# Router logits scaled inside attention by a row of scales read back from DRAM, and two gated tiles finished by VectorE in the experts

## The reference

```python
x = x + tanh(g_xattn) * cross_attention(layernorm(x), ctx)   # 4 heads, 64 context tokens
x = x + tanh(g_ffn)   * experts(layernorm(x))
# experts, on groups of 32 tokens (n groups, t = 32), 32 experts x 4 sets = 128 columns
logits = einsum('bntd,des->bntes', grouped, Wc) + bc + tie
perm   = (logits == max(logits over t))                      # each expert picks one token of a group
inner  = relu(einsum(picked, W1) + b1)
result = einsum(inner, W2) + b2, scattered back with perm
```

## Time and profile before

| | |
|---|---|
| median of 3 runs | 1808.31 us (1807.01 to 1816.78) |
| profiled execution, its own time | 1809.33 us |
| its span | 1807.4 us |
| granted TensorE clock, mean | 0.971 |
| busy share PE / PEld / DVE / ACT / POOL | 91% / 63% / 71% / 42% / 48% |
| chain that ended last, by engine | PE 59%, DVE 11%, issue 10%, DMA 9%, POOL 8% |
| of it, DMA `gat<-r_scratch` / POOL L1219 / POOL L184 | 6% / 4% / 2% |
| DMA | 324.81 MB, mean 180 GB/s |

### The profile page before, as it was taken

One profiled execution on the slowest core, in us unless ns is written; L12 is line 12 of the kernel. 1 busy time (PEld: TensorE's weight loads), 2 busy tenths in 40 slices (PEclk: granted clock), 3 DMA queues, 4 the chain that ended last, 5 costly groups with the idle time before them and its releaser, 6 DMA issues.

```text
span 1807.4 us, 51758 instructions
## 1 busy us (share of the span) xinstructions
PE 1648.8 (91%) x22488; PEld 1146.4 (63%) x22488; DVE 1278.0 (71%) x1856; ACT 754.4 (42%) x995; POOL 858.6 (48%) x1016
## 2 busy tenths in 40 slices
PE   7899999999999999999779988888888888889896
PEld 4677777777777777777545665456644566445663
DVE  5677777777777777777537777666766767666676
ACT  3533232332333323322245545555455554555553
POOL 3467777767777677776322223332223322333213
PEclk9999999999999999999889999999899999999998
DMA  7534444444443445444457778786678766788666
GB/s 274 161 108 151 168 156 148 137 163 143 156 158 131 163 146 177 140 149 138 145 191 198 227 179 219 213 218 206 173 210 229 215 207 175 213 226 227 204 182 164
DMA packets 180882, 324.81 MB, mean 180 GB/s; under 512 B 23344, under 2 KB 33328, under 8 KB 179248
## 3 DMA queue, kind: packets, MB, share of 16 engines
q1 hardware_dynamic: 135728, 239.68, 40.5%
q0 software_dynamic: 17280, 31.46, 10.7%
q10 hardware_dynamic: 27648, 50.34, 8.1%
HBM read 242.71 MB, written 78.71 MB: 178 GB/s over the span
## 4 chain that ended last, share of the span: by engine, by line
PE 59%; DVE 11%; issue 10%; DMA 9%; POOL 8%; ACT 2%; SPq 1%; ACTq 1%; POOLq 0%; DVEq 0%
PE ps L1385 13%; PE ps L877 10%; PE ps L924 10%; PE ps L1358 7%; DMA gat<-r_scratch 6%; PE ps L937 5%; POOL out L1219 4%; PE ps L892 3%; PE ps L950 2%; DVE mx L675 2%; POOL xin L184 2%; PE ps L911 2%; PE ps L1408 2%; DVE lg L679 1%; DVE sm L684 1%
## 5 line engine op out<-in xcount | busy, mean ns | idle before, releaser
L184 POOL TENSOR_SCALAR xin<-xin,r_all,nb_all 128x512 f32<-128x512 f32 x128 | 97.9, 771 | 505.2 <-DMA xin<-out 505.1
L1298 DVE STREAM_TRANSPOSE res<-res 128x2048 f32<-128x2048 f32 x128 | 292.1, 2295 | 0.1
L1249 ACT ACTIVATE gat<-ps 128x1536 f32<-128x1536 f32 (+1 forms) x128 | 171.3, 1345 | 215.6 <-PE ps L1358 215.5
L1314 DVE COPY res<-ps 128x1024 f32<-128x1024 f32 x128 | 155.3, 1223 | 92.0 <-PE ps L1408 92.0
L877 PE MATMUL ps<-xTh,qh 128*128 128x512 f32 x512 | 208.9, 408 | 5.6 <-DVE qs L692 1.9
L877 PE MATMUL ps<-xTh,ql 128*128 128x512 f32 x512 | 200.3, 391 | 0.0
L877 PE MATMUL ps<-xTl,qh 128*128 128x512 f32 x512 | 200.0, 391 | 0.0
L1358 PE MATMUL ps<-sel,xin 32*128 32x128 f32 x4096 | 158.2, 293 | 37.4 <-POOL xin L184 17.2
L1263 ACT ACTIVATE res<-ps 128x1024 f32<-128x1024 f32 x128 | 131.2, 1025 | 143.6 <-PE ps L1408 143.6
L532 POOL TENSOR_TENSOR qc<-qc,qs 128x512 f32<-128x512 f32 x64 | 82.6, 1290 | 208.8 <-DVE qs L692 208.8
L1358 PEld LDWEIGHTS ps<-sel,xin 32*128 32x128 f32 x4096 | 135.7, 197 | 50.6 <-issue 25.5
(11 more groups left out here) (156 smaller groups left out, 3376.3 us busy)
## 6 DMA issues: line engine op xcount, KB each, us to landing
gat<-in_W ACTq DMA_DIRECT2D x192, 256.0 KB, 6.6
xT<-in_xT SPq DMA_DIRECT2D x32, 1024.0 KB, 6.2
xin<-in_x SPq DMA_DIRECT2D x64, 512.0 KB, 3.8
out<-xin SPq DMA_DIRECT2D x64, 512.0 KB, 3.8
xin<-out SPq DMA_DIRECT2D x128, 256.0 KB, 4.5
xin<-in_W SPq DMA_DIRECT2D x128, 256.0 KB, 3.5
out<-xin POOLq DMA_DIRECT2D x120, 256.0 KB, 7.6
xT<-in_W SPq DMA_DIRECT2D x68, 256.0 KB, 4.4
```

The costliest lines, as they stand in the source:

```text
L184: e.tensor_scalar(self.xn[:, t, :], self.xn[:, t, :], self.r[:, i, t:t + 1], self.nb[:, i, t:t + 1], ALU.mult, ALU.add).then_inc(self.m_xn ...
L1249: e.activation(o, v, ACT.Copy).then_inc(m_gaA.sem, 1)
L1298: e.transpose(v, v).then_inc(m_tr.sem, 1)
L1314: e.tensor_copy(o, v).then_inc(m_evV.sem, 1)
```

## The change

One more slot for `lx` (three), a buffer `rrow` for the scales in attention, and `rowk` moves from the stage-wide constants to the experts. SyncE's `store_r` becomes `logits_out`: it stores r, waits for that, loads r back from DRAM broadcast to all partitions, waits for GpSimd's product, and stores the scaled logits. In the experts the load of r and the product are gone, and VectorE makes tiles 0 and 1 of `finish` between its picks.

```diff
+LX_RING = 3
     def load_logits(self, e, i, h):
-        v = self.room(i, h)
-        e.dma_start(v[:, 0:HT], self.lg_dram[i, h]).then_inc(self.d_lg[h].sem, 16)
-        e.dma_start(v[:, HT:2 * HT], self.r_dram[i, h].rearrange("p t -> (p t)").partition_broadcast(P)).then_inc(self.d_lg[h].sem, 16)
+        e.dma_start(self.room(i, h)[:, 0:HT], self.lg_dram[i, h]).then_inc(self.d_lg[h].sem, 16)
...
-    def scaled(self, e, i, h):
...
-            e.wait_ge(self.m_lr.sem, self.m_lr.at(i, h))
+            e.wait_ge(self.d_lg[h].sem, self.d_lg[h].at(i))
...
-        lx = sb("lx", [P, 2, HT])
+        lx = sb("lx", [P, LX_RING, HT])
+        rrow = sb("rrow", [P, HT])
...
         def sync(e):
-            def store_r(u):
-                e.wait_ge(route.m_r.sem, route.m_r.at(u // 2, u % 2))
-                e.dma_start(route.r_dram[u // 2, u % 2], route.r[:, u // 2, u % 2 * TH:(u % 2 + 1) * TH]).then_inc(d_r.sem, 16)
+            def logits_out(u):
+
+                i, h = u // 2, u % 2
+                e.wait_ge(route.m_r.sem, route.m_r.at(i, h))
+                e.dma_start(route.r_dram[i, h], route.r[:, i, h * TH:(h + 1) * TH]).then_inc(d_r.sem, 16)
+                e.wait_ge(d_r.sem, d_r.at(u))
+                e.dma_start(rrow[:], route.r_dram[i, h].rearrange("p t -> (p t)").partition_broadcast(P)).then_inc(d_rr.sem, 16)
+                e.wait_ge(m_lsr.sem, m_lsr.at(u))
+                e.dma_start(route.lg_dram[i, h], lx[:, u % LX_RING, :]).then_inc(d_lgs[u % LX_RING].sem, 16)
...
-                e.wait_ge(m_ls.sem, m_ls.at(u))
-                e.dma_start(route.lg_dram[u // 2, u % 2], lx[:, u % 2, :]).then_inc(d_lgs[u % 2].sem, 16)
...
                     if h and u:
-                        store_r(u - 1)
+                        logits_out(u - 1)
...
-            store_r(NU - 1)
+            logits_out(NU - 1)
...
-            for k in range(2):
-                e.wait_ge(d_lgs[k].sem, d_lgs[k].at(B - 1))
-            e.wait_ge(d_r.sem, d_r.at(NU - 1))
+            for k in range(LX_RING):
+                e.wait_ge(d_lgs[k].sem, d_lgs[k].at((NU - 1 - k) // LX_RING))
...
         def gpsimd(e):
+            def scaled_logits(u):
+                o = lx[:, u % LX_RING, :].rearrange("p (t s) -> p t s", s=P)
+                e.wait_ge(m_ls.sem, m_ls.at(u))
+                e.wait_ge(d_rr.sem, d_rr.at(u))
+                e.tensor_tensor(o, o, rrow[:].rearrange("p (s t) -> p t s", t=TH), ALU.mult).then_inc(m_lsr.sem, 1)
...
                                         rc[:, tp, :].unsqueeze(2).broadcast_to([P, 8, S]), ALU.mult).then_inc(m_pr.sem, 1)
+                if unit(g - 2):
+                    scaled_logits(g - 2)
                 if unit(g + 1):
                     rotated(g + 1, 0)
...
-                if g == NU - 1:
-                    route.scaled(e, 0, 0)
-                    route.scaled(e, 0, 1)
                 if g >= NU - 2:
                     for t in range(TH):
                         route.normed(e, 0, (g - NU + 2) * TH + t)
+            scaled_logits(NU - 2)
             row_scale(NU - 1)
+            scaled_logits(NU - 1)
...
             def part_of_x(u):
                 e.wait_ge(m_LX.sem, m_LX.at(u))
-                if u >= 2:
-                    e.wait_ge(d_lgs[u % 2].sem, d_lgs[u % 2].at(u // 2 - 1))
-                e.activation(lx[:, u % 2, :], ps[:, 7, :], ACT.Copy).then_inc(m_lx.sem, 1)
+                if u >= LX_RING:
+                    e.wait_ge(d_lgs[u % LX_RING].sem, d_lgs[u % LX_RING].at(u // LX_RING - 1))
+                e.activation(lx[:, u % LX_RING, :], ps[:, 7, :], ACT.Copy).then_inc(m_lx.sem, 1)
...
+        def finish(e, i, t):
+
+            e.wait_ge(m_sc.sem, m_sc.at(i, t))
+            if t < 2:
+                e.tensor_scalar(tile_of(t), ps[:, 4 + t % 4, :], gate_f[:], None, ALU.mult).then_inc(m_finV.sem, 1)
+            else:
+                e.activation(tile_of(t), ps[:, 4 + t % 4, :], ACT.Copy, scale=gate_f[:]).then_inc(m_fin.sem, 1)
...
-                    route.scaled(e, i + 1, 0)
-                    route.scaled(e, i + 1, 1)
...
                         for h in range(2):
-                            for step in range(3):
-                                pick(i + 1, h, step)
+                            pick(i + 1, h, 0)
+                            if live(i - 1) and h == 0:
+                                finish(e, i - 1, 0)
+                            pick(i + 1, h, 1)
+                            if live(i - 1) and h == 0:
+                                finish(e, i - 1, 1)
+                            pick(i + 1, h, 2)
```

More of the change, by code:

```diff
@@ L91, in build @@
         b2s = sb0("b2s", [P, 2, D], F32R)
-        rowk = sb0("rowk", [P, 4, P], F32R)
         part = sb0("part", [P, 18])
         tie = sb0("tie", [P, G])
-        consts = (bcol, b1r, b2s, rowk, part, tie)
+        consts = (bcol, b1r, b2s, part, tie)
         const_loads = [(bcol, bc), (tie, tie_in.partition_broadcast(P)), (part, part_in)]
@@ L162, in __init__ @@
         self.d_x = [mark(f"x{t}", 1, 16) for t in range(NT)]
-        self.d_lg, self.m_r = [mark(f"dlg{h}", 2, 16) for h in range(2)], mark("r", 2)
-        self.m_xn, self.m_lr, self.m_log, self.m_mx, self.m_eq = mark("xn", NT), mark("lr", 2), mark("log", 2), mark("mx", 2), mark("eq", 2)
+        self.d_lg, self.m_r = [mark(f"dlg{h}", 1, 16) for h in range(2)], mark("r", 2)
+        self.m_xn, self.m_log, self.m_mx, self.m_eq = mark("xn", NT), mark("log", 2), mark("mx", 2), mark("eq", 2)
         self.m_sT, self.m_sel = mark("sT", 2), mark("sel", 2)
@@ L238, in attention @@
     nhalf, none_, eps_l, eps_r = small
-    b2s, rowk, part = consts[2:5]
+    b2s, part = consts[2:4]
     st = ExitStack()
@@ L333, in attention @@
         m_vcp, m_vce = pmark("vcp", NC), pmark("vce", NC)
-        d_vc, d_lgs, d_r = mark("dvc", 1, 16), [mark(f"lgs{k}", 1, 16) for k in range(2)], mark("dr", 1, 16)
-        m_vch, m_vcl, m_LX, m_LP, m_lx, m_ls = (mark(n) for n in ("vch", "vcl", "LX", "LP", "lx", "ls"))
+        d_vc, d_lgs, d_r, d_rr = mark("dvc", 1, 16), [mark(f"lgs{k}", 1, 16) for k in range(LX_RING)], mark("dr", 1, 16), mark("drr", 1, 16)
+        m_vch, m_vcl, m_LX, m_LP, m_lx, m_ls, m_lsr = (mark(n) for n in ("vch", "vcl", "LX", "LP", "lx", "ls", "lsr"))
         m_s1, m_ag1, m_r1 = mark("s1", TH), mark("ag1"), mark("r1", 3)
@@ L1056, in experts @@
         NY = TH
-        bcol, b1r, b2s, rowk, part, tie = consts
+        bcol, b1r, b2s, part, tie = consts
         xn = route.xn
@@ L1062, in experts @@
         res = sb("res", [P, Q * D])
+        rowk = sb("rowk", [P, 4, P], F32R)
         spare = lambda i: gat[:, 1, i % 2 * UW:(i % 2 + 1) * UW]
@@ L1073, in experts @@
         m_gaA, m_hr, m_evA = mark("gaA", 2 * C), mark("hr", 8), mark("evA", 8)
-        m_gaV, m_evV, m_tr, m_fin = mark("gaV", 2 * C), mark("evV", 8), mark("tr", 8), mark("fin", NT)
+        m_gaV, m_evV, m_tr, m_fin = mark("gaV", 2 * C), mark("evV", 8), mark("tr", 8), mark("fin", NT - 2)
         d_last = mark("last", 4, 16)
         m_gate, m_add, m_end = mark("gate", 3), mark("add", 3), mark("end", 2)
+        m_row = mark("row")
+        m_finV = mark("finV", 2)
         m_xn, m_sel = route.m_xn, route.m_sel
@@ L1143, in copied, with finished @@
             e.wait_ge(m_evV.sem, m_evV.at(i, u))
+        def finish(e, i, t):
[4 more added lines that the diff above has]
+                e.activation(tile_of(t), ps[:, 4 + t % 4, :], ACT.Copy, scale=gate_f[:]).then_inc(m_fin.sem, 1)
+        def finished(e, i, t):
+            m, k = (m_finV, t) if t < 2 else (m_fin, t - 2)
+            e.wait_ge(m.sem, m.at(i, k))
         def load_second(e, i, u, c):
@@ L1268, in scalar @@
                         copy(i, n)
+                    if i == 0:
+                        e.activation(rowk[:].rearrange("p u (k n) -> p (u k) n", k=4), part[:, 0:16].unsqueeze(2).broadcast_to([P, 16, NG]),
+                                     ACT.Copy).then_inc(m_row.sem, 1)
                     for c in range(QUARTERS):
@@ L1276, in scalar @@
                 for t in range(NT):
-                    if live(i - 1) and i < B:
-                        finish(i - 1, t)
+                    if live(i - 1) and i < B and t >= 2:
+                        finish(e, i - 1, t)
                     if live(i) and t < QUARTERS:
@@ L1327, in vector @@
                         for h in range(2):
-                            for step in range(3):
-                                pick(i + 1, h, step)
+                            pick(i + 1, h, 0)
[5 more added lines that the diff above has]
+                            pick(i + 1, h, 2)
+                    elif u == 0 and live(i - 1) and i < B:
+                        for t in range(2):
+                            finish(e, i - 1, t)
                     if live(i):
@@ L1415, in scatter @@
                 if t >= 4:
[L1416 removed]
+                    finished(e, i, t - 4)
                 elif t == 0 and live(i + 1):
```

19 lines of the change are left out of this document (5 added, 14 removed).

## The result

The changed kernel takes 1887.69 us (median of 4 runs, 1885.88 to 1898.05), the kernel before 1807.66 us (4 runs, 1799.24 to 1816.78). The ratio is 1.045, interval 1.039 to 1.052: slower by 80 us. The forecast was slower by 35, 1843 us, and its range ended at 1880. The direction was right, the size was not.

What follows compares the result with a forecast made beforehand. TensorE's order was taken to bound attention; in the experts, TensorE near its limit alternated with late GpSimd products and DMA. Attention +71, hand-over +15, experts -51 on 1809.3 gave 1844, put at 1843 for the median; range 1803 to 1880.

Steps and rivals of the forecast that it cites:

- No slack in the third slot: Attention: the logits copy waits within one turn for r, its DRAM trip, product and store; 29 copies wait, +71 us.
- wait-hidden rival: Attention: the third slot does give a unit of slack, leaving +15 - 51, 1772 us; chance 0.04.
- A to rotation: Attention: from A, the start of ScalarE's copy of the logits, to the rotation, now A+4.4 instead of A+5.0.
- rotation to r: Attention: 12.8 us from rotation until r is made, at A+17.2, up to 0.7 later in units with the `vol` part.
- r's landing: Attention: r lands in DRAM behind the x store on the same queue, 0.7 earlier than A+21.0, at A+20.3.
- store of the logits: Attention: the 256 KB store after the product takes 2.0 us, then the copy starts again at A+24.15+L.
- L: Attention: time of the broadcast load of r's row from DRAM, taken as 3.3 us, between 2.6 and 4.2.
- product: Attention: GpSimd's scaling of the logits after the row load, 1.65 us and 0.05 of release.
- The clock as a second cause: Rival "more on both sides": attention +97 with L 4.2, TensorE's clock low after idling, experts -36; 1886 us, chance 0.07.
- Hand-over: Attention to experts: two round trips of r now precede the load of ring[1], +15 us (13.5 to 16.7).
- long L: Attention: the row load at 4.2 us, making attention +97 us.
- Experts: Two loads, two GpSimd products and their wait go per batch; 3.6 us each for 14, 1 for the last: -51 (-23 to -88).

Runs made afterwards that it cites:

- experiment 2: Changed kernel with ten more TensorE matmuls, results unused, per unit where it waits for the copy of the logits; 1891.71 us, 1.048 of the kernel before.
- experiments 4 and 5: Changed kernel with x's second-half store behind r's store and row load: 1846.24 us; changed kernel with only a quarter of turned x loaded in later units: 1843.52 us.
- experiment 7: The changed kernel's experts on the attention of the kernel before, logits stored unscaled; 1764.99 us, 0.977 of the kernel before.

## Why the prediction missed

- **No slack in the third slot: right.** 29 copies were released by the store, unit by unit. The wait-hidden rival is out.
- **A to rotation, rotation to r: right.** 17.2 forecast, 17.4 measured; the difference is the `vol` part in every second unit, which the sum named and did not add.
- **r's landing: this step failed.** It was put as "Everything ahead of it on the queue moves with the rotation or with `values`, 0.6 to 1.0 earlier; I take 0.7: A+20.3." Measured: A+21.5. The 1.2 us are three pieces: 0.3 since the one unit I read (r at A+21.0) was better than the mean before (A+21.3), 0.7 of expected gain that did not come, and 0.2 later still. Times 29, that is 34 of the 38.5 missing us; most of the rest is the store of the logits, 2.16 where the sum had 2.0. The x store ahead of r was issued 0.7 earlier, as said (at A+12.7, 13.4 before), only in 12 units, all with TensorE at 1.00; in the 16 at 0.94 it went out 0.9 later, at A+14.3. Over all 29 it landed at A+21.1 (A+20.9 before). Even an earlier issue is not an earlier landing: experiment 2 has the issue 0.7 earlier and no gain, and experiments 4 and 5 show that the landing is set by the 512 KB store and the 1 MB load in flight together.
- **L, product: right.** L was 3.3 in the mean, as taken, between 2.6 and 4.2. The Trainium skill, DMA: Bandwidth & Descriptors, "Anatomy of one DMA", comes to an estimate of 2.6 for the size; that section's figures are for DMAs that GpSimd issues, and this load is SyncE's. The shortest of the 32 row loads in the changed kernel took 3.0. The end of 4.2 was real as well, at the hand-over (4.43 and 4.04) and wherever r's store was quick.
- **The clock as a second cause: the symptom right, the price open.** The prediction allowed for slow matmuls after TensorE's idle time, as "1 to 2 us of that fit behind the loop, more would show". They did show: at 0.94 the `values` matmuls end later, the x store goes out later, and the unit is 1.1 us longer, 16 times; an estimate from these means is 18 us of the missing 38.5, inside the late landing above. Yet with the clock held up (experiment 2) the time did not change, so no run shows these 18 us given back. The Trainium skill, TensorE: Matmul & The Clock Gate, "HAM oscillation", has it that a kernel that idles in every turn can be throttled in every turn; the trace agrees in part, with 16 turns of 29. That 1886 was this rival's number is luck: its L of 4.2 and its 36 us from the experts did not come.
- **Hand-over: right,** +16.7 for 15. **Experts: right in the mechanism,** -52.5 for -51; the scatter-to-gather stretch was put at about 25 and took 25.02. The accumulating DMAs took longer to land than the 6 to 8 given, and the start 8 us sooner paid for it. That the sum came within 2 us is in part luck, as experiment 7 shows (34 to 47 us). The two loads' bytes stand in the prediction at 1.4 us a batch and then as 1.6 in the range; only the range's -23 hangs on that.
- **The range** was too narrow on the slow side. Its attention term moved only with L; the landing of r, an extrapolation of one row by an argument on order, had no bounds of its own. With 0 to 0.7 of gain there, and the mean A+21.3 in place of one unit, the sum is 1851 to 1872, and the long L takes its end past the result.

## What to carry to other kernels

A round trip through DRAM that must close within one turn of a loop costs its full length over the slack, times the turns; counting the buffers against the distance between producer and user shows this before any run. Price a small transfer by when the bytes in flight with it land, not by when it or they are issued, and from a mean over turns. A faster trip gave back 1.5 to 1.7 us a unit and a warmer clock nothing; moving the waiting instruction behind those that did not need it gave 3.4.

## What the runs showed of the hardware

- A 2 KB store and the 128-way row load behind it did not shorten independently. Over the nine profiles with per-unit trips, the 74 loads behind a store of under 1.5 us took 4.0 us in the median (3.6 to 5.7), the 147 behind a store of 3 us or more 3.1 (3.0 to 4.4). This held on ScalarE's queue too (1.4 and 4.3 in one unit), and with nothing else in flight on SyncE's. The 67 in between took 3.5. Why is open; no run here parts it.
- TensorE idle for 2.1 to 2.9 us in a unit, as in nearly all of the 29, had its granted clock at 0.94 in 16 of 29 units and at 1.00 in the rest. With ten more matmuls in that idle time it was 1.00 in 26 of 29.
- A 2 KB store issued while a 1 MB load and a 512 KB store were in flight took 3.4 us in the median on an otherwise empty queue, 4.4 behind them on the same one. At its quickest it took 1.4.
